# Four attention heads side by side in row groups, a new order of every engine in part one, and four scan states moved into the next pass

## The reference, cut to what matters

```python
# block 0
h = layernorm(x) * (1 + ca) + sa
k, q = ln16(h @ Wk.T), ln16(h @ Wq.T)      # layer norm inside each of 16 heads of 16 features
v = h @ Wv.T
dot = einsum(q, k) / 4, masked above the diagonal with -inf
x = x + ga * (softmax(dot) @ v) @ Wu.T
h = layernorm(x) * (1 + cb) + sb
x = x + gb * ternary_ffn(h)                # 256 -> 1024 (twice) -> 1024 -> 1024 -> 256
# block 1
h = layernorm(x) * (1 + ca) + sa
xp, z = split(h @ W_in); dlt, Bm, Cm = split(xp @ W_xproj)
delta = clip(softplus(dlt @ W_dt + b_dt), 0.001, 0.1)
for each position t:                       # 512 channels x 16 states
    hs = (1 + A * delta_t) * hs + B_t * delta_t * xp_t
    y_t = sum over states of C_t * hs
x = x + ga * ((y + D * xp) * silu(z)) @ W_out
x = x + gb * (fp6_quantized(layernorm(x) * (1 + cb) + sb) @ quantized(W).T + bias)
```

## Time and profile before

| what | value |
|---|---|
| median of 3 runs | 5517.21 us (5516.57 to 5517.29) |
| the profiled execution's own time | 5520.1 us |
| its span, first to last instruction | 5518.3 us |
| busy share: PE, DVE, ACT, POOL | 77%, 71%, 50%, 45% |
| one loop pass, start to start (968.4 to 1295.9) | 327.5 us |
| of it part one and part two | 185.4 and 142.1 us |

### The profile page before, as it was taken

One profiled execution on the slowest core, in us unless ns is written; L12 is line 12 of the kernel. 1 busy time (PEld: TensorE's weight loads), 2 busy tenths in 40 slices (PEclk: granted clock), 3 DMA queues, 4 the chain that ended last, 5 costly groups with the idle time before them and its releaser, 6 DMA issues. The chain is left out here.

```text
span 5518.3 us, 55172 instructions
## 1 busy us (share of the span) xinstructions
PE 4276.4 (77%) x15853; PEld 2706.3 (49%) x15853; DVE 3917.5 (71%) x6879; ACT 2735.8 (50%) x5566; POOL 2464.7 (45%) x2070
## 2 busy tenths in 40 slices
PE   6887887887778877778887778788777887777833
PEld 4555555454455545445554455545445554544511
DVE  4427778585876948678684877858587694867876
ACT  3435455454545545454554645545454554545432
POOL 1224536263463625436362553626346362543633
PEclk9999999999999999999999999999999999999965
DMA  4510102010020201102020110201002020110200
GB/s 170 187 50 28 62 5 77 12 62 32 20 74 1 81 12 47 46 8 85 1 77 16 33 61 5 77 12 62 32 20 74 1 81 12 47 47 8 73 4 4
DMA packets 69381, 248.65 MB, mean 45 GB/s; under 512 B 9456, under 2 KB 9840, under 8 KB 68592
## 3 DMA queue, kind: packets, MB, share of 16 engines
q1 hardware_dynamic: 68976, 243.67, 13.0%
HBM read 212.19 MB, written 31.46 MB: 44 GB/s over the span
## 5 line engine op out<-in xcount | busy, mean ns | idle before, releaser
L1248 POOL TENSOR_TENSOR kept<-kept,hb 128x512 f32<-128x512 f32 x768 | 970.0, 1286 | 387.9 <-DVE hb L1195 387.9
L903 ACT ACTIVATE room<-ps,row_min 128x128 f32<-128x128 f32 (+3 forms) x1024 | 539.6, 527 | 1103.4 <-DVE row_min L963 1102.4
L963 DVE CUSTOM_DVE_ANT_0 ps<-ps,causal 128x128 f32<-128x128 f32 (+3 forms) x1024 | 506.0, 494 | 672.7 <-PE ps L818 670.8
L1188 DVE TENSOR_TENSOR_SCAN hb<-a_bar,ps 128x512 f32<-128x512 f32 x768 | 895.2, 1211 | 0.0
L767 POOL TENSOR_SCALAR room<-room,head_mask 128x512 f32<-128x512 f32 x208 | 344.4, 1656 | 1116.6 <-PE ps L818 1075.4
L818 PE MATMUL ps<-room 128*128 128x128 f32 (+3 forms) x2048 | 738.7, 444 | 94.7 <-ACT room L903 62.6
L1043 PE MATMUL ps<-hid_bhi,wring 128*128 128x512 f32 x1536 | 635.4, 414 | 154.6 <-issue 130.0
L840 PE MATMUL ps<-room 128*128 128x512 f32 (+3 forms) x2048 | 732.7, 444 | 0.8 <-issue 0.8
L829 PE MATMUL ps<-ident,room 128*128 128x128 f32 x2560 | 475.7, 285 | 278.1 <-ACT room L903 276.6
L1043 PE MATMUL ps<-hid_blo,wring 128*128 128x512 f32 x1536 | 625.0, 407 | 0.0
L1128 ACT ACTIVATE a_bar<-kept,a_neg 128x512 f32<-128x512 f32 x768 | 493.8, 715 | 167.3 <-PEq L740 104.8
(11 more groups left out here) (179 smaller groups left out, 7308.5 us busy)
## 6 DMA issues: line engine op xcount, KB each, us to landing
wring<-w_hi SPq DMA_DIRECT2D x352, 512.0 KB, 3.3
kept<-in_wffn SPq DMA_DIRECT2D x22, 512.0 KB, 4.2
w_hi<-wring SPq DMA_DIRECT2D x22, 512.0 KB, 2.6
w_lo<-wrest SPq DMA_DIRECT2D x22, 512.0 KB, 2.9
xn<-in_x_fm SPq DMA_DIRECT2D x17, 512.0 KB, 3.2
out_fm<-xc SPq DMA_DIRECT2D x16, 512.0 KB, 2.6
room<-in_wmod SPq DMA_DIRECT2D x2, 1536.0 KB, 7.9
win<-in_win SPq DMA_DIRECT2D x1, 1024.0 KB, 8.9
```

The source lines that it names most:

```text
L903: act.activation(probs[:, h % 2, TRI[j]:TRI[j + 1]], bank(n % 2)[:, 0:(j + 1) * P], ACT.Exp, bias=row_min[:, n:n + 1], scale=-1.0, accum_o ...
L963: dve.tensor_tensor_reduce(bank(n % 2)[:, 0:w], bank(n % 2)[:, 0:w], causal[:, T - w:T], 1.0, 3.0e38, ALU.add, ALU.min, row_min[:, n:n + 1 ...
L1188: dve.tensor_tensor_scan(hb[:, s % 8, :], a_bar[:, s % 6, :], bank(2 + m % 2), 0.0, ALU.mult, ALU.add).then_inc(scanned, 1)
L1248: pool.tensor_tensor(acc[:, m, :], acc[:, m, :], hb[:, s % 8, :], ALU.add).then_inc(acc_done, 1)
```

## The change

1. Attention works on four heads at a time ("quads"). The weight columns don't change, but two versions of queries and keys are kept (`q_ver`, `k_ver`), in which only the even or only the odd heads of each 32-row group are left. A head's scores are a matmul over 32 rows, and four heads in four row groups write to banks 0 to 3. Scores are made twice: once as before, with a causal product of the identity and a mask matrix added, only for the row's maximum (`find_max`, one reduction over four heads); the negated maxima are turned and added into a free row of the query (`shift_q`), and then transposed scores with the maximum already subtracted (`scores_turned`), of which one exponential covers four heads (`exp_probs`). So the 160 turns and the copies are gone. POOL zeroes the blocks on the diagonal (`causal_probs`). `values` uses 32 columns per head, four heads to four column groups of bank 4; a column of ones gives the sums.
2. Head norms use a product with a block matrix (`head_mat`) in place of reductions and turns.
3. In part one every engine's order is an explicit list of calls.
4. States 12 to 15 run at the beginning of the next pass's part one, in place of states 0 to 3 late in the same pass; part two holds states 0 to 11. There are 12 states there before and after. `pre` no longer waits for early states.
5. In every state two chunks go through VectorE and POOL as one 1024-wide instruction. The decay of the second chunk has a zero in its first column, so that the scan starts anew there.

```diff
+QUADS = 4
+S_GROUPS = [[(3, 0)], [(2, 0), (0, 384)], [(1, 0)]]
+T_GROUPS = [[(0, 0)], [(1, 0), (3, 384)], [(2, 0)]]
+G_WIDTH = [512, 512, 256]
...
+                    def causal_probs(quad, u):
+                        if att:
+                            for j, at in T_GROUPS[u]:
+                                pool.wait_ge(exp_done, 3 * quad + u + 1)
+                                blk = probs[u][:, :, at:at + P]
+                                pool.affine_select(blk, blk, [[0, 4], [1, P]], ALU.is_ge, 0.0, base=0, channel_multiplier=-1).then_inc(p_masked, 1)
...
+                    def scores(quad, u):
+                        if not att:
+                            return
+                        c, p = quad // 2, quad % 2
+                        if quad == 0:
+                            if u == 0:
+                                pe.wait_ge(ver_ready, 8)
+                            else:
+                                pe.wait_ge(max_ready, u)
+                        elif u == 0:
+                            pe.wait_ge(q_shifted, quad)
+                        else:
+                            pe.wait_ge(exp_done, 3 * (quad - 1) + u)
+                        for i, at in S_GROUPS[u]:
+                            w = (i + 1) * P
+                            for g in range(4):
+                                r = slice(32 * g, 32 * g + 32)
+                                pe.matmul(bank(g)[:, at:at + w], q_ver[r, p, c, i * P:(i + 1) * P], k_ver[r, p, c, 0:w], start=True, stop=False)
+                            for g in range(4):
+                                mm = pe.matmul(bank(g)[:, at + i * P:at + w], ident_r[:, :], causal_r[:, :], start=False, stop=True)
+                        mm.then_inc(s_done, 1)
...
+                        if quad + 1 < QUADS:
+                            pe.wait_ge(max_ready, 3 * (quad + 1) + u + 1)
+                        elif u >= 1:
+                            pe.wait_ge(exp_done, 3 * quad + u)
+                        if u == 0:
+                            pe.wait_ge(q_shifted, quad + 1)
+                        for j, at in T_GROUPS[u]:
+                            w = T - j * P
+                            for g in range(4):
+                                r = slice(32 * g, 32 * g + 32)
+                                mm = pe.matmul(bank(g)[:, at:at + w], k_ver[r, p, c, j * P:(j + 1) * P], q_ver[r, p, c, j * P:T], start=True, stop=True)
+                        mm.then_inc(st_done, 1)
...
+                        for j, at in T_GROUPS[u]:
+                            w = T - j * P
+                            for g, h in enumerate(heads_of(quad)):
+                                mm = pe.matmul(bank(4)[32 * g:32 * g + 32, j * P:T], v_pad[:, j, h, :], probs[u][:, g, at:at + w],
+                                               start=(j == 0), stop=(j == 2))
+                        mm.then_inc(pv_done, 1)
...
+                                ins = dve.tensor_reduce(cols, ps[:, 0:4, at:at + (i + 1) * P], AX.X, ALU.max, negate=True)
+                            ins.then_inc(max_ready, 1)
...
+                            act.activation(probs[u], ps[:, 0:4, 0:G_WIDTH[u]], ACT.Exp).then_inc(exp_done, 1)
```

A stretch of TensorE's list, around the second quad, and of VectorE's:

```diff
+                    scores(1, 1)
+                    tail_spread(0, 3)
+                    values(0, 0)
+                    scores_turned(0, 1)
+                    x_proj()
+                    scores(1, 2)
+                    tail_spread(1, 3)
+                    values(0, 1)
+                    scores_turned(0, 2)
+                    dt_proj(0)
+                    turn_max(1)
+                    values(0, 2)
+                    scores(2, 0)
+                    row_sums(0)
...
+                    tail_in(2, 0)
+                    tail_in(2, 1)
+                    tail_scan(2, 0)
+                    tail_scan(2, 1)
+                    tail_out(2, 0)
+                    find_max(1, 1)
+                    split(8, 9)
+                    tail_out(2, 1)
```

Part two, a state:

```diff
-                                dve.tensor_tensor(bank(2 + m % 2), u[:, m, :], bank(0), ALU.mult).then_inc(b_ready, 1)
...
-                                dve.tensor_tensor_scan(hb[:, s % 8, :], a_bar[:, s % 6, :], bank(2 + m % 2), 0.0, ALU.mult,
-                                                       ALU.add).then_inc(scanned, 1)
...
+                            dve.tensor_tensor(ps[:, 2:4, :], u[:, 2 * h:2 * h + 2, :], spread_b, ALU.mult).then_inc(b_ready, 2)
+                            works(n, 3 * h)
...
+                            dve.wait_ge(a_ready, s + 2)
+                            dve.wait_ge(b_ready, s + 2)
+                            pair = hb[:, s % 8:s % 8 + 2, :]
+                            dve.tensor_tensor_scan(pair.rearrange("p a t -> p (a t)"), a_bar[:, s % 6:s % 6 + 2, :].rearrange("p a t -> p (a t)"),
+                                                   ps[:, 2:4, :].rearrange("p a t -> p (a t)"), 0.0, ALU.mult, ALU.add).then_inc(scanned, 2)
+                            works(n, 3 * h + 1)
                             dve.wait_ge(c_spread, n + 1)
...
+                            dve.wait_ge(scanned, s + 2)
+                            dve.tensor_tensor(pair, pair, spread_c, ALU.mult).then_inc(y_ready, 2)
```

More of the change, by code:

```diff
@@ L777, in _ @@
+                    causal_probs(3, 2)
+                    quant_at(1, 12)
+                    spread_sums(3)
                 @block.tensor
                 def _(pe):
[L779 to L787 removed]
@@ new lines, in _ @@
+                    project_v(1)
+                    gate_in(1)
+                    tail_spread(0, 1)
+                    scores(0, 1)
+                    gate_in(2)
+                    gate_in(3)
+                    tail_spread(1, 1)
+                    scores(0, 2)
+                    turn_max(0)
+                    tail_spread(0, 2)
+                    scores(1, 0)
+                    in_proj(0)
+                    in_proj(1)
+                    scores_turned(0, 0)
+                    tail_spread(1, 2)
@@ new lines, in _ @@
+                    row_sums(0)
+                    dt_proj(1)
+                    scores_turned(1, 0)
+                    dt_proj(2)
+                    dt_proj(3)
+                    scores(2, 1)
+                    out_proj(0)
+                    turn_sums(0)
+                    scores_turned(1, 1)
+                    out_proj(1)
+                    scores(2, 2)
+                    values(1, 0)
+                    scores_turned(1, 2)
+                    values(1, 1)
+                    fin_mean()
@@ new lines, in _ @@
+                    turn_max(2)
+                    scores(3, 0)
+                    values(1, 2)
+                    fin_var()
+                    row_sums(1)
+                    scores_turned(2, 0)
+                    scores(3, 1)
+                    turn_sums(1)
+                    values(2, 0)
+                    scores_turned(2, 1)
+                    fin_turn(0)
+                    fin_turn(1)
+                    scores(3, 2)
+                    values(2, 1)
+                    scores_turned(2, 2)
@@ new lines, in _ @@
+                    turn_max(3)
+                    values(2, 2)
+                    scores_turned(3, 0)
+                    row_sums(2)
+                    scores_turned(3, 1)
+                    turn_sums(2)
+                    values(3, 0)
+                    scores_turned(3, 2)
+                    values(3, 1)
+                    fin_back(0)
+                    att_proj(0)
+                    values(3, 2)
+                    att_proj(1)
+                    row_sums(3)
+                    att_proj(2)
@@ L859, in _ @@
+                    turn_sums(3)
+                    fin_back(1)
+                    fin_ff(0)
+                    fin_ff(1)
+                    att_proj(3)
                 @block.scalar
                 def _(act):
[L861 to L868 removed]
@@ new lines, in _ @@
+                    tail_scan(0, 1)
+                    normalise(0)
+                    normalise(1)
+                    normalise(2)
+                    normalise(3)
+                    tail_out(0, 0)
+                    tail_out(0, 1)
+                    find_max(0, 0)
+                    split(0, 1)
+                    pre_scale()
+                    tail_in(1, 0)
+                    tail_scan(1, 0)
+                    find_max(0, 1)
+                    split(2, 3)
+                    tail_in(1, 1)
@@ L988, in build @@
+                    invert(2)
+                    quant_at(1, 0, 1, 2)
+                    weigh(2)
+                    quant_at(1, 4, 5, 6, 7, 8, 9, 10, 11)
+                    invert(3)
+                    weigh(3)
+                    ff_add(0)
+                    ff_add(1)
+                    att_add(0)
+                    att_add(1)
         UNITS = 3 * HM + DC
+        NB = NS - TAIL
         def part_b(b, ffn, scan, k_ffn, k_next, has_rest):
-            first = EARLY if scan else 0
@@ L1141, in _ @@
```

(4 more changed lines are left out.)

1241 lines of the change are left out of this document (688 added, 553 removed).

## The result

The changed kernel takes 5419.01 us (median of 4 runs, 5413.8 to 5424.48), the kernel before in the same session 5516.89 us (5515.18 to 5517.29). The ratio is 0.9823, 95% interval 0.9808 to 0.9837: 98 us less. The forecast was 5400 us. The profiled run took 5417.0 us, with a span of 5415.2.

A forecast was written before the change was run, and what follows sets the result against it. No engine full: part one leans on TensorE in a ring of waits, part two on VectorE. 5520.1 - 146 + 42 - 25 + 10 = 5401, said as 5400 us; own range 5250 to 5560, overall 5000 to 5700.

The forecast's parts named there:

- rival 1: Part one's attention: four heads truly run together, TensorE's 64 us falls to 26 to 36; total 5150 us; chance 0.35.
- the signs named for being wrong: Part one under 165 or over 185 us, or DVE as its bound, or part two shorter than 142 us.
- Part one, TensorE's attention: Scores, transposed scores and values in a loop pass: partial overlap, 64 us in place of 102 without any.
- Part one, the waits: Loop part one: 145 us of TensorE work plus waits gives 175 us against 185.4, -146 us over 14 passes.
- The walk along the queue: Part one, PE's list walked with prices: first scores 22 us, quads 0 to 3 20, 35, 32, 34, end 32.
- Part two: Merged 1024-wide instructions make a half state 4.72 us instead of 4.61, 24 halves in 16 parts: +42 us.
- Pass 0: Bound by DMA, so 0 us (-5 to +15), since DVE and ACT stop for two tiles at once.
- Pass 1: No "fin", so PE loses 24 us and DVE its tails: 169.6 to some 145 us, -25.
- Passes 16 and 17: Start, tail of 38 us, then the "fin" chain: 94 us each; -22 and +31, together +10.
- Rivals 2 and 3: Part one: nothing runs together, 5850 us (chance 0.15); queued steps wait for each other, 20 us more per pass, 5680 (0.05).
- Rival 4: The 1024-wide scan isn't taken as one, or part two gains instead: -42 to -110 us; no separate chance given.
- the ring of banks 0 to 3: Part one: banks handed round from scores to maximum, previous quad's transposed scores, exponential, next scores; walked for the waits.

The follow-up runs named there:

- the doubled product: Changed kernel with every product of the transposed scores made twice, a head's second right behind its first: 5529.37 us, ratio to the kernel before 1.0022.
- the mends: Changed kernel with part two in single chunks, later store wait, unread products in part one's waits, and pass 0's weight split spread: 5155.31 us, ratio to before 0.9341.

## Why the prediction was right, and where it was not

The sign, the range and the total were right, the parts were not, and that the total came within 19 us is luck: what happened on TensorE is rival 1's mechanism, and its gain was eaten by waits, by the clock and by everything outside part one of the loop. None of the signs named for being wrong came up (part one under 165 or over 185 us, VectorE as its bound, part two under 142), but the eight records of `scores_turned` stood near rival 1's 0.9 us and not at 2.1.

- **Part one, TensorE's attention: this is the step that failed.** The prediction said that of a head's two records "the second must follow the first; if records start in program order, only the second of one head and the first of the next can run together", hence 64 us. In the run eight records of four heads take 1.07 us, a factor of 3.2; 102 us / 3.2 = 32 us. The flaw was the assumed order: records of different row groups do not queue behind each other, not even where the program writes one group's two products together (the doubled product). The Trainium skill (TensorE: Matmul & The Clock Gate, Part 3: Packing small matmuls) gave 3.07x, and I put it aside for an argument from record counts; the trace agrees with its factor (3.2). For its sentence that matmuls start and end in program order, the doubled product shows that the order does not keep groups from overtaking each other by a record.
- **Part one, the waits: the mirror error.** With 32 us instead of 64, TensorE's work is 113 us of 168.8, so 56 us are something else, where I had 30 (175 - 145). Its busy time is 135.75 us: 33 are idle, and as 39 us of the busy time are at the lower clock, where the same work takes nearly twice as long, some 20 are the price of the clock. Of the 32 us saved only 6 reached the end. Rival 1 had this mechanism, but said that half of it would turn into waits; it was four fifths. The walk along the queue looks good: scores of quad 0, 1, 2 and 3 stand 25, 45, 79 and 106 us after the pass's first product, against 22, 42, 77 and 109 forecast, and `tail_spread(0, 3)` waits 3.58 us for 3.7. But it fits with too much work in it and too little waiting. What it missed is the clock: it had the low clock only at the start of the pass, while in the run it falls again behind the waits in quad 3 that the walk itself lists, and with these waits filled it stays up (0.69 to 1.00).
- **Part two: right in kind, too small.** A half was forecast at 4.72 us, from two instructions of 512 columns with 0.13 us per dependent wait. It is 4.91: the wait after a 1024-wide instruction is 0.21. And the store's wait (3.3 us per pass, 2.0 of them the wait and the rest the clock behind it) was not seen at all: the prediction has no term for it, and the store is now the last thing before a barrier. Merging costs 4.3 us per pass, the store 3.3; 7.6 explains the measured 7.4.
- **Pass 0**: forecast 0 with +15 at most, measured +28. The named reason (two tiles at a time) was right; its price is the round trip of 12 us a step. Spread out, the part takes less than before the change.
- **Pass 1**: -34 for -25. That it is the same overlap, with no tail or "fin" to wait for, is likely but was not tested.
- **Passes 16 and 17**: +47 for +10. In the last pass, with little beside them, tail states take 11.7 us each, where I used 38 us for all four: 9 of the 12 us by which that pass missed its 94. Part one of pass 16 takes 117.6 us, 11.4 more than the last pass, from which it differs by the work of "pre", for which the forecast had charged nothing. There VectorE's next multiply waits four times for GpSimd's sum, 5.9 us in all; one of them:

```profile
5332.04 1.22 DVE L1106 TENSOR_TENSOR hb<-kept,ps 128x1024 f32<-128x1024 f32 x1 [1.49 <-POOL kept L524]
```

- **Others**: GpSimd's mask of 512 elements takes 0.73 us where I had taken 1.5; it cost nothing at the end, since GpSimd is busy 45.6 of 168.8 us.
- **Rivals 2 and 3** fell: nothing like 205 us, and no extra 20. Rival 4 fell too: the 1024-wide scan is taken as one (2.29 us).

**What stays open**: how much of the remaining 33 idle us in part one is the ring of banks 0 to 3 alone, the 29 us by which the mends more than add, and what in pass 0 is the split's order and what the clock.

## What to carry to other kernels

Where an engine's work is cut, price the silence too: here TensorE's clock fell to its lower level behind waits of 1 to 3 us each few microseconds, and products that nobody reads, placed in those waits, gave 86 us back, while the same products elsewhere cost 163. One longer wait at a barrier cost 2.0 us of idleness and 1.5 us more in the slower products behind it. Merging two instructions into one paid here only where the next instruction did not need the result (1.14 us for 1.19, but 1.35 where it did); look for what stood between them. After each reordering, read what now stands last before a barrier, and what a small setup task (here the weight split) paces when its steps are taken in pairs.

## What the hardware showed that I had not expected

- Matmuls over 32 of the 128 rows in four row groups advance independently of each other: 8 records take 1.07 us and 16, written in pairs of one group, 1.95, where 8 full ones take 3.43.
- An instruction of VectorE that waits for the one just before it starts 0.21 us later than one that does not, at 1024 columns (1.35 against 1.14).
- A small VectorE copy is held up beside GpSimd's memset. In the changed kernel three copies of 12 columns take 1.67 us while a memset of 2048 columns runs:

```profile
1272.06 1.80 POOL L498 MEMSET room<- 128x2048 f32 x1
```

```profile
1272.25 1.67 DVE L1087 COPY m<-mod 128x12 f32 x3 [1.76 <-PEq L1597]
```

In pass 0 of the kernel before, one copy of 12 columns takes 3.50 us, beside a memset of 3.51:

```profile
62.52 3.51 POOL L752 MEMSET room<- 128x4096 f32 x1 [13.97 <-POOLq L1254]
```

```profile
62.56 3.50 DVE L925 COPY m<-mod 128x12 f32<-128x12 f32 x1 [1.21 <-PEq L1254]
```

Where no long memset runs beside it, in the last pass of the changed kernel, the same copy takes 0.17 us.
